# Feed-forward part of a transformer layer rebuilt as seven products of quarter matrices, on eight cores

## The chip, the cores and the metric

The kernel runs on one Trainium2 chip, on all 8 of its cores. Each core does the whole layer for one of 8 batch elements, so there is no traffic between cores. The metric is the device time of the slowest core in microseconds (us), lower is better.

## The reference

One layer on `x` of 8 x 2048 x 1024 in float32: causal attention in which keys and values come from one weight matrix and the queries are `x` itself, then a feed-forward part with a token shift, each followed by a layer norm.

```python
kv = x @ W.T;  K, V = kv[..., :d], kv[..., d:]
scores = einsum('bqd,bkd->bqk', x, K) + mask
x = _layernorm(x + (x + einsum('bqk,bkd->bqd', softmax(scores), V)))
...
x_prev = concatenate([zeros, x[:, :-1, :]], axis=1)
xr = mu_r * x + (1.0 - mu_r) * x_prev
xk = mu_k * x + (1.0 - mu_k) * x_prev
r = sigmoid(einsum('btc,dc->btd', xr, W_r))
k_act = square(relu(einsum('btc,dc->btd', xk, W_k)))
x = _layernorm(x + r * einsum('btc,dc->btd', k_act, W_v))
```

Per core this is three products of 2048 x 1024 x 1024 for the feed-forward part, two for K and V, and the causal half of two of 2048 x 2048 x 1024.

## The kernel before

Every float32 operand is held as two bf16 halves, a high part (a cast on ScalarE) and a low part (value minus high part, on VectorE, helper `minus`, L501). A product is three matmuls, high x high, high x low and low x high, `triple`, lines L317 to L319. The five engine programs are written out by hand; each runs its list in order and waits on semaphores.

**Projection.** Sixteen steps `ss` of 96 matmuls make K and V for four blocks `tt` of 512 tokens. Results go to PSUM banks 0 to 3 or 4 to 7 in turn, are split by `high_p` and `low_p`, and step `ss + 2` waits for `low_p(ss)`. Inputs come through NST = 6 staging buffers `STG` of 256 KB: SyncE (SP) issues load n once the cast of load n - 6 is done (L199).

**Attention.** Rows of 128 queries, q = 15 down to 0. TensorE flips the probabilities (L388, `flip_p`), does the scores of row q - 1, and then probabilities times V of row q (L474 to L479), with the normalized row q + 1 flipped in between (L397, `flip_x`). VectorE has row maxima (`row_max`), the low halves of the flipped probabilities (`low_p_t`), the end of the row before (`attn_rows`: L576, L578 and the variance; `normal`, L568), and, by the tables CASTS, MIXES and TILES, at the end of some rows the casts of later operands and the token mixes. GpSimd makes the token difference (`change`, L273) in `X1T`, 1/sqrt of the variance (L262), and issues the stores of `x1` and its transpose `x1t`.

**Feed-forward.** `ffn_tile(g)`, 96 tiles of 24 matmuls: for each block of 512 tokens 8 tiles of keys, 8 of the gate, 8 of values. All three weights stay in SBUF as bf16 halves (`FK`, `FR`, `FV`). The first tiles are put between the last attention rows: TILES = {3: (0, 1), 2: (1, 2), 1: (2, 4), 0: (4, 6)}. The first tile on `XR` waits for all its mixes (`v_mix`) and for `FR`. Each tile's PSUM bank is freed by one operation of ScalarE or VectorE. After the last tile: L667 gate times value, L671 residual, L561 to L564 variance, L262, L568, store.

Of the kernel before, what the change touches and what calls it, by code (L numbers as in the profile page):

```python
# [18 lines left out]
NST = 6  # L19


def build_program():
# [13 lines left out]
    x1t_d = nc.dram_tensor("x1t", [D, S], F32, kind="Internal").ap()  # L36
# [10 lines left out]
    oA, oB, oC, oD, oE = 0, 32 * KB, 64 * KB, 96 * KB, 128 * KB  # L47
    oF = 160 * KB
    oG = oF + 16 * KB + 32
    oST = oG + 16 * KB  # L50
    oX = oST + NST * 2 * KB
    oM = oX + 2 * KB
# [10 lines left out]
    STG = [at(f"STG{i}", [128, 512], F32, oST + i * 2 * KB) for i in range(NST)]  # L63
# [4 lines left out]
    XTS = [at(f"XTS{i}", [128, 512], F32, oD + 24 * KB + i * 2 * KB) for i in range(2)]  # L68
    MA = [at(f"MA{i}", [128, 512], F32, o) for i, o in enumerate((oD + 20 * KB, oD + 22 * KB, oX))]

    FK, FR, FV = hilo("FK", 8, 1024, oC), hilo("FR", 8, 1024, oB), hilo("FV", 8, 1024, oA)
    XK, XR = hilo("XK", 8, 512, oE), hilo("XR", 8, 512, oE + 16 * KB)
    X1T = at("X1T", [128, 8 * 513], F32, oF).rearrange("p (c w) -> p c w", w=513)
    KA = hilo("KA", 8, 512, oG)
    R = at("R", [128, 4 * 1024], F32, oD).rearrange("p (c w) -> p c w", w=1024)
    X1 = [at(f"X1_{i}", [128, 1024], F32, oD + 16 * KB + i * 4 * KB) for i in range(3)]
    KT = [at(f"KT{i}", [128, 512], F32, oD + 28 * KB + i * 2 * KB) for i in range(2)]
    MB = [at(f"MB{i}", [128, 512], F32, oST + i * 2 * KB) for i in range(3)]
# [16 lines left out]
    nc.const_aps.register(F32, 0.0, CONST0.ap())  # L95

# [11 lines left out]
    ld_xt = sem("ld_xt")  # L108
    ld_x1, st_y = ([sem(f"{n}{i}") for i in range(3)] for n in ("ld_x1", "st_y"))

    pe_p, pe_s, pe_t, pe_pv, pe_f = sem("pe_p"), sem("pe_s"), sem("pe_t"), sem("pe_pv"), sem("pe_f")
# [4 lines left out]
    v_mx, v_mix, v_sq, v_ka = sem("v_mx"), sem("v_mix"), sem("v_sq"), sem("v_ka")  # L116
    v_v, v_y, v_init = sem("v_v"), sem("v_y"), sem("v_init")

    a_st, a_p, a_pt, a_exp = sem("a_st"), sem("a_p"), sem("a_pt"), sem("a_exp")
    a_xt, a_mh, a_r, a_k, a_kh = sem("a_xt"), sem("a_mh"), sem("a_r"), sem("a_k"), sem("a_kh")  # L120

    g_rs, g_d, g_zero = sem("g_rs"), sem("g_d"), sem("g_zero")
# [3 lines left out]
    def chunk(n):  # L126

        def xs(tt, cc, x):
            return x0_d[cc * 128:(cc + 1) * 128, tt * 512:(tt + 1) * 512], x[0][:, cc, :], x[1][:, cc, :]

        def ws(d, h, cc, w):
            c = slice(h * 512, (h + 1) * 512)
            return d[cc * 128:(cc + 1) * 128, c], w[0][:, cc, c], w[1][:, cc, c]

        cc = n % 8
        if n < 24:
            return xs(0, n // 3, XP[0]) if n % 3 == 0 else ws(wk_d, n % 3 - 1, n // 3, WK)
# [13 lines left out]
    MIXES = {9: (0, 3), 8: (3, 6), 7: (6, 8), 1: (8, 10), 0: (10, 13)}
    TILES = {3: (0, 1), 2: (1, 2), 1: (2, 4), 0: (4, 6)}
# [9 lines left out]
    def first(q):  # L162

        return sum(G(p) for p in range(q + 1, NQ))
# [4 lines left out]


    def t_p(q, g):
        return first(q) + 2 * max(0, NQ - 2 - q) + g

    def t_x(q, i):
        return (t_p(q - 1, 0) + G(q - 1) if q > 0 else 70) + i

    t_kind = {t_p(q, g): ("p", first(q) + g) for q in range(NQ) for g in range(G(q))}
    t_kind.update({t_x(q, i): ("x", 2 * (NQ - 1 - q) + i) for q in range(NQ) for i in range(2)})

    def mix_dst(n):  # L180

        return (XK if n // 8 % 2 == 0 else XR), n % 8, (MUK if n // 8 % 2 == 0 else MUR)

    def mtmp(n):
        return (MA if n < 24 else MB)[n % 3]


    def bank(g):
        return 1 + g % 3 if g < 8 else (3, 0, 6, 7, 1, 2, 4, 5)[g % 8]

    def gate_tile(j):

        return j % 4, j // 4


    def sync_program(sy):
        def load(n):
# [10 lines left out]
        for n in range(4, 86):  # L208
            load(n)
# [13 lines left out]
        for n in range(86, N_WV):  # L223
            load(n)
# [624 lines left out]
```

## Time and profile before

| quantity | value |
|---|---|
| median of 3 runs | 1291.97 us (1273.01, 1291.97, 1403.23) |
| the profiled execution's own time | 1272.16 us |
| its span, slowest core (core 5) | 1270.6 us |
| spans of the eight cores | 1262.6 to 1270.6 us |
| granted TensorE clock, mean by core | 0.986 to 0.990 of full |
| TensorE busy | 1224.5 us, 96% |
| VectorE, ScalarE, GpSimd busy | 38%, 21%, 11% |

Time and span of the profiled execution differ by 1.56 us, which lies around the span. In the trace a matmul's duration includes its way through the array, so the distance from one start to the next is what it costs, not its duration.

### The profile page before, as it was taken

To read this page: it belongs to the slowest core of one execution; us is meant where nothing else is said; L and a number is where in the kernel's file an instruction comes from. 1 tells how busy PE (TensorE), PEld (TensorE's weight loads), DVE (VectorE), ACT (ScalarE), POOL (GpSimd) and SP (SyncE) were. 2 spreads that over 40 slices of the span, in tenths; PEclk is the share of its full clock that TensorE was granted. 3 is DMA by queue.
4 is the path that set the end of the run, shared out by engine and by line. 5 is a ranking of instruction groups with operands and counts; after the bars stand their busy time and mean duration, and the time that the engine had idled before them with its cause. 6 is when DMAs were issued, how large, how long until landed. Compare 5 with 4: busy or idle time off the path is not lost.

```text
span 1270.6 us, 15768 instructions; the slowest of 8 cores (1262.6 to 1270.6 us)
## 1 busy us (share of the span) xinstructions
PE 1224.5 (96%) x5880; PEld 579.0 (46%) x5880; DVE 481.3 (38%) x810; ACT 271.2 (21%) x514; POOL 139.9 (11%) x165
## 2 busy tenths in 40 slices
PE   7999999999999999999989996799999999999997
PEld 3444444444445554555445553344444444444443
DVE  4532121010112232332475667367432832382024
ACT  4431121010112121221233332341221122112100
POOL 0000000000000011111231223222111211120000
PEclk9999999999999999999989998899999999999999
DMA  7622020000101021323144661452300230021002
GB/s 207 179 67 67 1 67 1 1 1 1 34 1 34 17 84 50 83 84 117 50 119 133 186 194 51 149 150 83 117 1 1 84 116 1 1 100 35 1 1 83
DMA packets 36172, 87.17 MB, mean 69 GB/s; under 512 B 4096, under 2 KB 4352, under 8 KB 36096
## 3 DMA queue, kind: packets, MB, share of 16 engines
q1 hardware_dynamic: 28928, 60.98, 16.7%
q0 software_dynamic: 7168, 25.17, 6.0%
q8 instruction: 48, 0.79, 0.3%
q14 instruction: 28, 0.23, 0.1%
HBM read 60.97 MB, written 25.17 MB: 68 GB/s over the span
## 4 chain that ended last, share of the span: by engine, by line
PE 88%; DVE 5%; issue 2%; ACT 2%; DMA 1%; POOL 1%; DVEq 0%; POOLq 0%; ACTq 0%; SPq 0%
PE ps L317 24%; PE ps L318 24%; PE ps L319 24%; PE ps L474 2%; PE ps L475 2%; PE ps L478 2%; PE ps L477 2%; PE ps L476 2%; PE ps L479 2%; DMA X1T<-x1t 1%; DVE MA L586 1%; PE ps L388 1%; PE ps L397 1%; POOL MA L273 1%; DVE BN L561 1%
## 5 line engine op out<-in xcount | busy, mean ns | idle before, releaser
L317 PE MATMUL ps<-FRH,XRH 128*128 128x512 bf16 x256 | 98.7, 386 | 15.2 <-DVE XRL L501 11.5
L318 PE MATMUL ps<-FRL,XRH 128*128 128x512 bf16 x256 | 98.7, 385 | 0.0
L319 PE MATMUL ps<-FRH,XRL 128*128 128x512 bf16 x256 | 98.3, 384 | 0.0
L317 PE MATMUL ps<-FVH,KAH 128*128 128x512 bf16 x256 | 97.0, 379 | 0.0
L318 PE MATMUL ps<-FVL,KAH 128*128 128x512 bf16 x256 | 97.0, 379 | 0.0
L319 PE MATMUL ps<-FVH,KAL 128*128 128x512 bf16 x256 | 97.0, 379 | 0.0
L319 PE MATMUL ps<-XKH,FKL 128*128 128x512 bf16 x256 | 97.0, 379 | 0.0
L318 PE MATMUL ps<-XKL,FKH 128*128 128x512 bf16 x256 | 97.0, 379 | 0.0
L317 PE MATMUL ps<-XKH,FKH 128*128 128x512 bf16 x256 | 97.0, 379 | 0.0
L262 POOL TENSOR_TENSOR RS<-VE,NEGH 128x1 f32<-128x1 f32 x32 | 23.3, 727 | 406.5 <-DVE VE L564 406.5
L721 ACT ACTIVATE PROB<-ps,NEGM 128x512 f32<-128x512 f32 (+3 forms) x40 | 24.8, 622 | 194.7 <-DVE NEGM L545 194.7
L273 POOL TENSOR_TENSOR MB<-X1T 128x512 f32<-128x512 f32 x40 | 47.5, 1199 | 130.6 <-DVE XKL L501 91.2
L501 DVE SCALAR_TENSOR_TENSOR PT<-PT,ps 128x512 bf16<-128x512 bf16 (+3 forms) x40 | 23.2, 604 | 89.6 <-ACT PT L729 89.6
L667 DVE TENSOR_TENSOR R<-R,ps 128x512 f32<-128x512 f32 x32 | 22.0, 687 | 90.2 <-PE ps L319 90.2
L258 POOL DMA_DIRECT2D Z<-xtok x16 | 9.1, 566 | 343.0 <-PE ps L319 342.3
L317 PEld LDWEIGHTS ps<-FRH,XRH 128*128 128x128 bf16 x256 | 25.4, 99 | 47.1 <-issue 18.0
L289 POOL DMA_DIRECT2D x1t<-XTS x32 | 24.5, 766 | 191.6 <-ACT XTS L736 190.7
L604 DVE TENSOR_TENSOR KT<-KT 128x512 f32<-128x512 f32 x32 | 22.8, 711 | 60.1 <-ACT KT L747 60.1
L542 DVE TENSOR_REDUCE MX<-ps 128x1 f32<-128x512 f32 (+3 forms) x40 | 24.5, 611 | 51.3 <-PE ps L319 49.7
L805 ACT ACTIVATE R<-ps 128x512 f32<-128x512 f32 x32 | 19.1, 596 | 103.0 <-PE ps L319 103.0
L741 ACT CAST XRH<-MB 128x512 bf16<-128x512 f32 x24 | 14.8, 618 | 121.3 <-DVE MB L586 121.3
L319 PEld LDWEIGHTS ps<-FRH,XRL 128*128 128x128 bf16 x256 | 25.4, 99 | 31.3 <-issue 1.9
(249 smaller groups left out, 2467.2 us busy)
## 6 DMA issues: line engine op xcount, KB each, us to landing
STG<-x SPq DMA_DIRECT2D x56, 256.0 KB, 6.0
Z<-xtok POOLq DMA_DIRECT2D x16, 512.0 KB, 6.1
x<-Z POOLq DMA_DIRECT2D x16, 512.0 KB, 3.0
x1t<-XTS POOLq DMA_DIRECT2D x32, 256.0 KB, 3.1
X<-x SPq DMA_DIRECT2D x16, 512.0 KB, 3.8
y<-X SPq DMA_DIRECT2D x16, 512.0 KB, 2.6
X1T<-x1t SPq DMA_DIRECT2D x3, 2052.0 KB, 14.0
STG<-wk SPq DMA_DIRECT2D x16, 256.0 KB, 5.7
```

The source lines that it names most:

```text
L273: gp.tensor_tensor(mtmp(n), X1T[:, cc, 1:513], X1T[:, cc, 0:512], op=ALU.subtract).then_inc(g_d, 1)
L289: gp.dma_start(out=dst, in_=XTS[i].rearrange("p (c s) -> p c s", s=128)).then_inc(st_xt[i], 16)
L317: te.matmul(out, a[0], b[0], start=at_first, stop=False)
L318: te.matmul(out, a[0], b[1], start=False, stop=False)
L319: return te.matmul(out, a[1], b[0], start=False, stop=at_last)
L474: te.matmul(PS[6], ph, vh[:, j, 0:512], start=beg, stop=False)
L475: te.matmul(PS[7], ph, vh[:, j, 512:1024], start=beg, stop=False)
L476: te.matmul(PS[6], ph, vl[:, j, 0:512], start=False, stop=False)
L477: te.matmul(PS[7], ph, vl[:, j, 512:1024], start=False, stop=False)
L478: te.matmul(PS[6], pl, vh[:, j, 0:512], start=False, stop=end)
L479: mm = te.matmul(PS[7], pl, vh[:, j, 512:1024], start=False, stop=end)
L721: sc.activation(out=PROB[:, g * 512:g * 512 + w], in_=PS[g][:, 0:w], func=AF.Exp, bias=NEGM, scale=1.0, accum_out=Z4[:, g:g + 1]).then_inc ...
```

## The change

**Products.** The contraction, the rows and the columns of each 1024-wide product are halved. Per stage and half of the block (n = 2b + u, 24 of them) seven products of quarters replace eight; `product(n, k)` is 24 matmuls of 128x512, or in the key stage 48 of 128x256. The results are added up from PSUM on VectorE (`u2`, `u3`, `u4`, `quarter`).

**Stages.** The feed-forward part now runs all key blocks (b = 0 to 3), then all gate blocks, then all value blocks. The squared keys and the gate go to device memory (`ka`, `r`) and come back.

**Weights.** Seven combinations of weight quarters, as halves, are made by `weight_unit`, 12 units of 128 rows: 8 in the projection, 4 in attention rows 12 to 9. They are stored to `wc` and loaded by stage in 7 slots (`load_slot`).

**Inputs.** Of each piece, four parts are cast as they are (768 columns hold the three first), and four sums (`sums`, on GpSimd, 4 additions of 128x256) are cast as 128x1024.

**Order.** The attention rows run 15 to 7, 3, 6, 2, 5, 1, 4, 0. The first two products stand ahead of the last row's values, and wait for their pieces tile by tile. `attn_rows` now comes ahead of the probabilities' low halves; the casts of sums come behind these. NST is 5. The last row is finished by halves of 512 columns.

```diff
-NST = 6
+NST = 5
+ORDER = [15, 14, 13, 12, 11, 10, 9, 8, 7, 3, 6, 2, 5, 1, 4, 0]
+    UNITS = {12: 8, 11: 9, 10: 10, 9: 11}
+    MIXES = {ORDER[8 + x]: x for x in range(4)}
+    PROD = {1: (2, 0), 2: (0, 1), 3: (6, 2), 4: (1, 6), 5: (3, 3), 6: (4, 4), 7: (5, 5)}
+    ORDER_P = (1, 2, 6, 7, 5, 4, 3)
...
+        def load(n):
+            if n >= NST:
+                old = CH[n - NST]
+                if old[0] == "st":
+                    sy.wait_ge(v_st, plain(n - NST))
+                elif old[0] == "m":
+                    sy.wait_ge(v_mx, old[2] + 1)
+                elif n - NST == N[f"u{old[2]}"][0]:
+                    store_unit(old[2])
...
+        def sums(x):
...
+            step(gp.tensor_tensor(s1, a21, a22, op=ALU.add))
+            gp.tensor_tensor(s3, a11, a21, op=ALU.subtract)
+            step(gp.tensor_tensor(s2, s1, a11, op=ALU.subtract))
+            gp.tensor_tensor(s4, a12, s2, op=ALU.subtract).then_inc(g_s, 1)
...
+        def product(n, k):
...
+            if turn < 4:
+                te.wait_ge(a_exp, 40)
+            elif turn < 6:
+                te.wait_ge(v_z, 16)
+            else:
+                product_read(te.wait_ge, (turn - 6) // 7, ORDER_P[(turn - 6) % 7])
+            ac = AC[b % 2]
+            for t in range(2 if s == 0 else 1):
+                for p in range(4):
+                    if k in (1, 2) and u == 0 and t == 0:
+                        te.wait_ge(v_ac, 8 * b + 2 * p + 1)
...
+        def weight_1(u):
...
+            step(ve.tensor_tensor(UT[:, 0:512], b12, b11, op=ALU.subtract))
+            ve.tensor_tensor(UT[:, 512:1024], b22, UT[:, 0:512], op=ALU.subtract).then_inc(v_ut, 1)
+            for m, f in enumerate((b11, b21, b22)):
+                ve.wait_ge(a_w, 5 * u + m + 1)
+                minus(ol[:, m, :], oh[:, m, :], f)
...
+            step(minus(flat(ol, 3, 5), flat(oh, 3, 5), UT))
+        def weight_2(u):
+            ve.tensor_tensor(UT[:, 0:512], b22, b12, op=ALU.subtract)
+            ve.tensor_tensor(UT[:, 512:1024], b21, UT[:, 512:1024], op=ALU.subtract).then_inc(v_ut, 1)
...
+            minus(flat(ol, 5, 7), flat(oh, 5, 7), UT).then_inc(v_w, 1)
...
         for q in ORDER:
+            prev, nxt = before(q), after(q)
+            if prev is not None:
+                attn_rows(prev)
+            low_p_t(q, 0)
...
+            if prev in MIXES:
+                low_unit(MIXES[prev])
...
+            if q in MIXES:
+                mix(MIXES[q])
```

TensorE, one key tile. Before, the first six of its 24 rows at `ffn_tile(0)` (eight such triples for one bank):

```order
L317 MATMUL ps1<-XKH_99,FKH_93 128x512
L318 MATMUL ps1<-XKL_100,FKH_93 128x512
L319 MATMUL ps1<-XKH_99,FKL_94 128x512
L317 MATMUL ps1<-XKH_99,FKH_93 128x512
L318 MATMUL ps1<-XKL_100,FKH_93 128x512
L319 MATMUL ps1<-XKH_99,FKL_94 128x512
```

After, the beginning of a key product (four such triples for each half of a bank; `AC` are the pieces, `WA` a slot of weights):

```order
L637 MATMUL ps0<-AC00H_114,WA0_100 128x256
L638 MATMUL ps0<-AC00L_115,WA0_100 128x256
L639 MATMUL ps0<-AC00H_114,WA0_100 128x256
L637 MATMUL ps0<-AC01H_116,WA0_100 128x256
L638 MATMUL ps0<-AC01L_117,WA0_100 128x256
L639 MATMUL ps0<-AC01H_116,WA0_100 128x256
```

The triples are the same, half as wide, and of half the depth.

SyncE in the projection. Before, its queue holds nothing but loads of `STG` there (x0 here, wk and wv ahead of it):

```order
L200 DMA STG3_80<-wv 128x512
L200 DMA STG4_81<-x0 128x512
L200 DMA STG5_82<-x0 128x512
L200 DMA STG0_77<-x0 128x512
L200 DMA STG1_78<-x0 128x512
```

After, each unit of weights has four loads (`fk` or `fr`) and two stores (`UO` are the made halves) in the same queue; the stores of unit 2 stand ahead of the last three loads of unit 3:

```order
L342 DMA STG1_78<-fk 128x512
L342 DMA STG2_79<-fk 128x512
L342 DMA STG3_80<-fk 128x512
L330 DMA wc<-UO65536H_90 128x7x512
L330 DMA wc<-UO65536L_91 128x7x512
L342 DMA STG4_81<-fk 128x512
L342 DMA STG0_77<-fk 128x512
L342 DMA STG1_78<-fk 128x512
L342 DMA STG2_79<-fr 128x512
```

The two stores stand between one unit's end and the next one's inputs.

VectorE at the end of attention. Before, between the flipping of row 1's results and those of row 0 (`Z0`):

```order
L568 TENSOR_SCALAR Z1_87<-Z1_87,MV0_126,RS0_130 128x1024
L604 TENSOR_TENSOR KT0_110<-KT0_110 128x512
L501 SCALAR_TENSOR_TENSOR KAL_105<-KAH_104,KT0_110 128x512
L604 TENSOR_TENSOR KT1_111<-KT1_111 128x512
L501 SCALAR_TENSOR_TENSOR KAL_105<-KAH_104,KT1_111 128x512
L586 SCALAR_TENSOR_TENSOR MA1_91<-MA1_91,MUR_117,X1T_103 128x512
L586 SCALAR_TENSOR_TENSOR MA2_92<-MA2_92,MUR_117,X1T_103 128x512
L501 SCALAR_TENSOR_TENSOR XRL_102<-XRH_101,MA1_91 128x512
L586 SCALAR_TENSOR_TENSOR MA0_90<-MA0_90,MUR_117,X1T_103 128x512
L501 SCALAR_TENSOR_TENSOR XRL_102<-XRH_101,MA2_92 128x512
L501 SCALAR_TENSOR_TENSOR XRL_102<-XRH_101,MA0_90 128x512
L576 SCALAR_TENSOR_TENSOR Z0_86<-ps6,RZ0_123,Z0_86 128x512
```

After, in the same place (row 4 is now the last but one; `OUT0` is the first quarter of a result, L970 a mix for the second block):

```order
L945 TENSOR_SCALAR Z0_85<-Z0_85,MV0_163,RS0_167 128x1024
L1018 TENSOR_TENSOR OUT0_138<-SN0_135,ps1 128x512
L954 SCALAR_TENSOR_TENSOR Z1_86<-ps6,RZ1_161,Z1_86 128x512
L956 SCALAR_TENSOR_TENSOR Z1_86<-ps7,RZ1_161,Z1_86 128x512
L970 SCALAR_TENSOR_TENSOR TP1_131<-TP1_131,MUK_155,STG4_81 128x512
```

Ten operations on keys and mixes are gone from there; one addition stands in their place, and the mixes come behind `Z`.

## Rows read from the trace of the kernel before

**Rows 1.** The page, busy time of the engines.

```profile
PE 1224.5 (96%) x5880; PEld 579.0 (46%) x5880; DVE 481.3 (38%) x810; ACT 271.2 (21%) x514; POOL 139.9 (11%) x165
```

**Rows 2.** Windows by stage: us, busy of each engine, PEclk, DMA share, GB/s.

```profile
0.00:343.00 343.00, 335.18 (x1540) 151.43 (x1541) 82.72 (x129) 75.63 (x129) 0.20 (x4) 1.00 0.20 55
343.00:716.50 373.50, 363.62 (x1884) 186.08 (x1882) 138.10 (x267) 78.67 (x178) 44.88 (x65) 0.99 0.26 77
716.50:830.00 113.50, 93.42 (x458) 45.67 (x457) 69.10 (x122) 39.18 (x75) 29.98 (x36) 0.91 0.47 142
830.00:1262.40 432.40, 432.28 (x2003) 195.82 (x2001) 187.51 (x288) 77.77 (x133) 64.30 (x59) 1.00 0.17 54
1262.40:1270.60 8.20, 0.00 (x0) 0.00 (x0) 3.84 (x7) 0.00 (x0) 0.55 (x1) 0.74 0.16 64
```

**Rows 3.** TensorE's groups by shape: nine such in the feed-forward part.

```profile
L317 PE MATMUL ps<-FRH,XRH 128*128 128x512 bf16 x256 | 98.7, 386 | 15.2 <-DVE XRL L501 11.5 <-DVE FRL L501 3.7
```

**Rows 4.** Timeline of TensorE, scores of row 13: start, duration, operation.

```profile
409.92 0.38 PE L317 MATMUL ps<-K0H,XP3H 128*128 128x512 bf16 x1
...
425.46 0.27 PE L317 MATMUL ps<-K3H,XP3H 128*128 128x256 bf16 x1
...
427.97 0.27 PE L319 MATMUL ps<-K3H,XP3L 128*128 128x256 bf16 x1
```

**Rows 5.** Timeline of TensorE, where it had been idle: the bracket has the idle time before.

```profile
7.83 0.59 PE L317 MATMUL ps<-XP0H,WKH 128*128 128x512 bf16 x1 [7.83 <-DVE WKL L501]
...
365.68 1.94 PE L388 MATMUL ps<-IDN,PROB 128*128 128x128 f32 x8 [2.60 <-ACT PROB L721]
...
622.19 0.38 PE L474 MATMUL ps<-V0H,PT 128*128 128x512 bf16 x1 [1.05 <-DVE Z L578]
...
650.43 0.59 PE L474 MATMUL ps<-V0H,PT 128*128 128x512 bf16 x1 [4.85 <-DVE Z L578]
...
723.46 0.41 PE L397 MATMUL ps<-IDN,Z 128*128 128x128 f32 x2 [1.49 <-DVE Z L568]
...
772.08 0.66 PE L397 MATMUL ps<-IDN,Z 128*128 128x128 f32 x2 [2.81 <-DVE Z L568]
...
797.67 0.58 PE L317 MATMUL ps<-FRH,XRH 128*128 128x512 bf16 x1 [11.54 <-DVE XRL L501]
...
825.31 0.38 PE L317 MATMUL ps<-FRH,XRH 128*128 128x512 bf16 x1 [3.71 <-DVE FRL L501]
```

**Rows 6.** Windows on TensorE: us, busy, PEclk, DMA share, GB/s.

```profile
652.00:656.00 4.00, 4.00 (x12) 0.58 0.14 59
800.00:804.00 4.00, 4.00 (x15) 0.74 0.52 145
0.00:50.00 50.00, 42.17 (x183) 1.00 0.79 213
```

**Rows 7.** Groups by shape on VectorE and ScalarE: count, busy us, mean ns, idle before.

```profile
L501 DVE SCALAR_TENSOR_TENSOR WKL<-WKH,STG 128x512 bf16<-128x512 bf16 x16 | 10.7, 691 | 3.1 <-ACT WKH L689 3.1
L604 DVE TENSOR_TENSOR KT<-KT 128x512 f32<-128x512 f32 x32 | 22.8, 711 | 60.1 <-ACT KT L747 60.1
L501 DVE SCALAR_TENSOR_TENSOR XQ0L<-XQ0H,STG 128x512 bf16<-128x512 bf16 x8 | 11.1, 1444 | 14.2 <-ACT XQ0H L689 14.2
...
L689 ACT CAST WKH<-STG 128x512 bf16<-128x512 f32 x16 | 9.8, 617 | 3.9 <-DMA STG<-wk 3.4
```

**Rows 8.** The instructions on `X1T`: count, ns min/median/max, first and last start.

```profile
L273 POOL TENSOR_TENSOR MB<-X1T x40: 1033/1117/1537, 846.6 to 1133.4; 128x512 f32<-128x512 f32 x40
...
L586 DVE SCALAR_TENSOR_TENSOR MA<-MA,MUK,X1T x16: 737/740/2436, 612.4 to 846.3; 128x512 f32<-128x512 f32 x16
```

**Rows 9.** The page, DMA issues: KB each, median us to landing.

```profile
STG<-x SPq DMA_DIRECT2D x56, 256.0 KB, 6.0
...
X1T<-x1t SPq DMA_DIRECT2D x3, 2052.0 KB, 14.0
```

More of the change, by code:

```diff
@@ L74, in build_program, with seven @@
[L74 to L78, printed above, removed]
+    XTS = [at(f"XTS{i}", [128, 512], F32, oD + 20 * KB + i * 2 * KB) for i in range(2)]
+    UT = at("UT", [128, 1024], F32, oX)
+    def seven(name, w, off):
+        return at(name, [128, 7 * w], BF16, off).rearrange("p (m w) -> p m w", w=w)
@@ L171, in t_p @@
     def t_p(q, g):
-        return first(q) + 2 * max(0, NQ - 2 - q) + g
+        return T_EV["p", q, g]
     def t_x(q, i):
[L175 to L185, printed above, removed]
@@ new lines, in pair_free, with store_unit @@
+    def pair_free(wait, x):
+        if x >= 6:
+            wait(v_ac, 2 * (x - 1))
+        elif x >= 4:
+            wait(pe_pv, first(4) + 2)
+        elif x > 0:
+            wait(v_ac, 2 * x)
+    def sync_program(sy):
+        def store_unit(u):
+            sy.wait_ge(v_w, u + 1)
+            o, p = unit_out(u), u % 4
+            for h in range(2):
+                dst = wc_d[u // 4, h, :, p * 128:(p + 1) * 128, :].rearrange("m p w -> p m w")
+                sy.dma_start(out=dst, in_=o[h]).then_inc(st_w, 16)
@@ L372, in scores, with exp_before @@
                 mm.then_inc(pe_s, 1)
+        def exp_before(q, g):
+            p = before(q)
+            while G(p) <= g:
+                p = before(p)
+            return first(p) + g + 1
         def bank_free(e):
@@ L454, in tensor_program @@
                 flip_p(q, 1)
-            if q > 0:
-                scores(q - 1)
-            if q in TILES:
-                for g in range(*TILES[q]):
-                    ffn_tile(g)
+            if q == 0:
+                product(0, 1)
+                product(0, 2)
+            else:
+                scores(after(q))
+            prev = before(q)
             for g in range(n):
@@ new lines, in vector_program @@
+        for b in range(1, 8):
+            x, n = 4 * b + 4, 2 * b
+            more = x < 32
+            if more:
+                mix(x)
+            quarter(b, 0)
+            low_unit(x)
+            u2(n)
+            if more:
+                mix(x + 1)
+            u3(n)
+            quarter(b, 1)
+            u4(n)
+            low_unit(x + 1)
+            quarter(b, 2)
+            if more:
+                mix(x + 2)
+            quarter(b, 3)
+            if more:
+                mix(x + 3)
+            low_unit(x + 2)
+            quarter(b, 4)
+            u2(n + 1)
+            low_unit(x + 3)
+            u3(n + 1)
+            quarter(b, 5)
+            u4(n + 1)
+            quarter(b, 6)
+            quarter(b, 7)
@@ L685, in scalar_program @@
+        ve.wait_ge(g_rs, 32)
+        for h in range(2):
+            part = x1[:, h * 512:(h + 1) * 512]
+            ve.tensor_scalar(part, part, MV[1][:, 0:1], RS[1], op0=ALU.subtract, op1=ALU.mult).then_inc(v_y, 1)
     def scalar_program(sc):
```

1145 lines of the change are left out of this document (776 added, 369 removed).

## The prediction

> **What bounds the kernel now.** I read the page first: TensorE is busy 96% of the span, the next engine 38% [rows 1]. Then the windows by stage: TensorE is full from 830 us to the last matmul at 1262.4, nearly full in projection and attention, and only 93.4 of 113.5 us are busy in the change-over from attention to feed-forward, where the granted clock also falls to 0.91 [rows 2]. Behind the last matmul come 8.2 us. So the time is a floor of matmuls plus the places where TensorE waits. The timeline gives both: starts are 0.2158 us apart for 128x512 (409.92 to 425.46, 72 of them) and 0.1091 us for 128x256 (425.46 to 427.97, 23 intervals) [rows 4]; and the idle times say who was late [rows 5].
>
> **Products.** The feed-forward part has nine groups of 256 matmuls [rows 3]: 2304 x 0.2158 = 497.2 us. By the order of the changed kernel, gate and value products have 16 x 7 x 12 = 1344 of 128x512 and the key products 8 x 7 x 24 = 1344 of 128x256: 290.0 + 146.6 = 436.7 us. That is 60.5 us less, all on the path, since no other engine is near its limit. A half-width matmul costs 0.0012 us more than half a full one, 1.6 us in all, which is in the sum.
>
> **What must stay hidden beside the products.** A product takes 5.2 us, a block of fourteen 72.6 us. A bank is taken again six products later, so a reader has some 26 us before TensorE waits. VectorE has per block in the key stage 8 mixes, 14 additions from PSUM, 4 casts of 768 and 4 of 1024 columns; at 0.69 us for 512 columns and in proportion for the wider ones [rows 7] that is 6 + 9.7 + 9.6 = 25 us of 72.6. ScalarE has 4 x (0.9 + 1.2) for casts and some 18 x 0.6 for the rest, 19 us [rows 7]. GpSimd has 8 differences at 1.12 us and 16 additions of 256 columns, which the trace does not show; between half of a 512-column one and all of it, 0.56 to 1.12 us [rows 8], they make 18 to 27 us. I take the half. In the value stage GpSimd has 8 residual additions in place of the differences, and no more. All fit by a factor of two or more. I cost them at nothing; if that cover were gone (a chain of mix, sums, two casts late by a block's time), it would be paid eleven times.
>
> **End of attention.** Six waits stand between 622 and 826 us: 1.05, 4.85, 1.49, 2.81, 11.54, 3.71, together 25.4 us [rows 5]. All name VectorE, and the order shows why: the mixes, key halves and weight casts of the first feed-forward block stood there between one row's results and the next. At the lower clock, 12 and 15 matmuls ran in 4 us where 18.5 fit [rows 6]; with the time from 650.43 and 797.67 to those windows at half speed, the two cost 2.2 and 2.0 us. For those behind 2.81 and 3.71 us of idleness I estimate 1 and 1.5 from these. So 32 us lie there. The changed kernel has its weights made long before; short rows alternate with long ones, so that scores (1.294 us for each 128 keys, 6 x 0.2158) cover the maxima and the exponential of the row ahead; and 10.4 us of products stand ahead of row 0's values. I followed the four iterations that carry a mix (rows 7, 3, 6, 2) with durations of rows 7 and 8. VectorE's tail there is casts 2.4 us, then two GpSimd differences 2.2 us that wait for these casts, then two mixes 1.5 us. In row 6 it ends 2.5 us before the values of that row are through. In row 2 it ends 2.6 us behind them; with the 1.5 us of `attn_rows` and 0.7 of `low_p_t` ahead of row 5's values, and 2.6 + 0.7 us of scores and flips beside it, TensorE waits about 1.5 us. Row 4, with only 1.4 us of scores beside it, gives 0.5. So of 32 us 30 are gained; what is late next there is VectorE again, by 2 us.
>
> For the additions that GpSimd now makes beside it: `XQ0L` took 1.44 us against 0.69, and a mix once 2.44 against 0.74, while GpSimd worked in the same stretch [rows 7, 8]. The Trainium skill, "SBUF — State Buffer", section "Who interferes with whom", says that a VectorE operation with two SBUF inputs and a GpSimd one that reads SBUF exclude each other, the later one waiting for the whole of the earlier. The doubled durations agree with it. By it each of the 24 GpSimd operations of those four rows (8 differences, 16 additions) could hold up VectorE by its own length, an estimate of 18 us of delay, of which TensorE would see only what falls in rows 2 and 5, some 5 us; that lies in the range.
>
> **Weights by units.** New work in the projection, where VectorE is busy 24% [rows 2]. A unit on VectorE: 4 additions x 0.71, 3 casts x 0.69, 2 of double width x 1.38, and one wait for a double cast of ScalarE, 1.23 [rows 7]: 8.9 us. Moved into SP's queue: two stores of 0.92 MB after each unit, ahead of the last three loads (0.79 MB) of the next. 2.62 MB at 213 GB/s, as in the first 50 us [rows 6], is 12.3 us. Period 21.2 us against 20.7 us (96 x 0.2158) for the projection step beside it. Behind VectorE's wait for those loads stands `low_p` of the next step, which may be late by about 15 us before step ss + 2 waits. Half a microsecond a unit over seven units is hidden. Queued too are the loads of the fourth token block, whose casts wait for the last stores into the same memory: I find them ready about when step 12 starts, and put 2 us there. The other bound is the transfer of 2052 KB in 14.0 us [rows 9], 150 GB/s: 17.5 + 8.9 = 26.4, 5.7 us late per unit, 40 over seven, of which 15 are hidden: 25 us. I take 2, since the issue pattern in the first 50 us is nearest (loads alone, one behind another). The stores' pieces of 1 KB in device memory occur nowhere in this trace.
>
> The Trainium skill, "DMA: Bandwidth & Descriptors", section "Specifications", gives line rate from 512 B up and 358 GB/s per core. By it the 2.62 MB would be an estimated 7.3 us and the period 16 us, with nothing lost; no run here has shown that rate for such a mix.
>
> The four units in attention rows 12 to 9 are split round a row maximum. A long row has 11 to 15 us of scores and as much of values: 8.9 us on VectorE fit, no cost.
>
> **Staging, start and end.** With 5 buffers of STG instead of 6 and 6.0 us to land [rows 9], plus 1.3 for the two casts [rows 7], a load comes each 1.5 us; TensorE needs one each 1.7 us (24 matmuls, 5.2 us, for three of them). The first wait of 7.83 and the one of 2.60 ahead of the first flip stay [rows 5]. I put 3 us for small waits here and at the joints of stages. At the end, an addition from PSUM (0.7) is added, half of the statistics and half of the normalization are taken off (0.7 + 0.4): 8.2 stays 8.
>
> **Sum.** 1270.6 - 60.5 - 32 + 2 (rows 5 and 4) + 2 (fourth block) + 3 = 1185.1 us of span, plus the 1.56 that lie around the span: 1187 us. The executions shown have a median of 1291.97 and a lowest of 1273.01; the sum is against the profiled one, 1272.16, which agrees with the lowest, and a changed kernel's median should be compared with that.
>
> **Rivals.**
> 1. *The units' transfers set the projection's pace.* For: the period is already 0.5 us over the step. Against: 15 us of slack, 213 GB/s reached by loads. Price 10 to 30 us: 1197 to 1217. Chance 0.15.
> 2. *The waits at the end of attention come back in a new place* (VectorE behind GpSimd in rows 3 to 5, or the casts of the first queries' block in row 8, which I find only 3 us early). For: the doubled durations. Price half of what I let go, 16 us, up to all of it: 1203 to 1219. Chance 0.13.
> 3. *The products do not run dense*: bank waits, late sums, or key products slower than 0.109 us per matmul. A wait of 1 us for each of 168 products would cost 168 us; for one in four, 42 us: 1229. Against: 26 us of slack each. Chance 0.05. Were it so throughout, the change would not do what it says.
> 4. *Slower than before.* The same mechanism as 1 with its threshold: the forecast is beaten by 85 us only if seven units are late by (85 + 15) / 7 = 14.3 us each, a period of 35 us, that is 2.62 MB in 26 us, under 100 GB/s. Then 1273 and more. The slowest large transfer in the rows has 150 GB/s. Chance 0.03.
>
> **How the numbers follow.** Forecast 0.64, alone 1176 (none of the 7 us of new waits, and the small waits under 0.6 us gone too) to 1196. Rivals 1 and 2 together go up to 1219. The range 1172 to 1220 leaves out rivals 3 and 4 and some tails. A difference under 2%, 25 us, could hardly be told from none. Faster by over 2% means under about 1247: 0.94; within 2%: 0.04; slower: 0.02.
>
> **What would show it.** In the profile after: 128x512 starts 0.216 us apart and 128x256 0.109 in the feed-forward part, which lasts about 437 us plus flips; TensorE above 97% busy; no idle time of 4 us or more between the start and the last matmul; DMA share roughly twice as high, with a GpSimd busy share near 20%; steps 4 to 12 of the projection without a wait on `low_p`. Wrong would be: TensorE idle with VectorE as releaser at steps 9 to 12 (rival 1), idle time at rows 3 to 4 (rival 2), or waits ahead of products beyond the first block (rival 3).

## The result and the profile after

The changed kernel takes 1224.74 us, median of six executions (1219.72 to 1229.9), against 1291.9 for the kernel before (lowest 1272.08). The ratio is 0.9625, 95% interval 0.9562 to 0.9687. All ratios, and the times of the experiments, leave out slow executions (over 1.5% above the fastest of the same kernel, or one die over 1% longer at a lower granted clock), without which the kernel before had 1268.5 to 1273.2 us beside every experiment. The profiled execution took 1224.53 us, with a span of 1223.0. That is faster by over 2%, but some 37.5 us above the forecast of 1187 and outside the range of 1172 to 1220.

The page of the changed kernel, busy time and then the chain that ended last:

```profile
PE 1166.1 (95%) x6264; PEld 614.1 (50%) x6264; DVE 624.4 (51%) x901; ACT 409.0 (33%) x673; POOL 369.4 (30%) x420
...
PE 59%; POOL 12%; DMA 10%; issue 7%; DVE 6%; ACT 3%; SPq 1%; DVEq 0%; POOLq 0%; ACTq 0%
```

TensorE's share has fallen from 96 to 95% [rows 1], and GpSimd has 369 us of work instead of 140. The chain is what to look at: only 59% of it is TensorE. The last matmul was held, step after step, by a chain that runs through GpSimd, DMA and VectorE.

Windows by stage (columns as in [rows 2]):

```profile
0.00:343.00 343.00, 335.84 (x1550) 152.03 (x1551) 137.67 (x202) 105.15 (x170) 3.51 (x9) 1.00 0.44 123
343.00:716.50 373.50, 368.43 (x1933) 190.14 (x1931) 164.91 (x315) 92.50 (x192) 59.43 (x86) 1.00 0.41 120
716.50:830.00 113.50, 104.36 (x894) 88.18 (x893) 73.14 (x97) 42.86 (x67) 67.53 (x70) 0.97 0.57 171
830.00:1060.00 230.00, 217.00 (x1258) 122.10 (x1257) 149.77 (x166) 86.25 (x121) 130.60 (x135) 0.99 0.53 157
1060.00:1215.00 155.00, 140.49 (x635) 61.61 (x633) 97.43 (x117) 80.30 (x122) 106.88 (x118) 0.99 0.56 195
1215.00:1223.00 8.00, 0.00 (x0) 0.00 (x0) 1.50 (x5) 1.97 (x3) 1.43 (x4) 0.50 0.33 131
```

Projection and attention went as forecast: TensorE lost 7.2 us in the first stage and 5.1 in the second, where it had lost 7.8 and 9.9 [rows 2]. In the change-over 104.4 of 113.5 us are busy instead of 93.4. Behind 830 us it is the other way round. There TensorE had been full (432.28 of 432.40); now it stands 13.0 us of the next 230 and 14.5 of the last 155, 3.1 of these behind the last matmul, which ends at 1211.9.

The chain of waits, by what TensorE waited for (us in total, times, longest):

```profile
PE ps L637 <- DVE OUT L1018: 18.3, 15, 3.9
PE ps L637 <- DVE WKL L825: 7.2, 1, 7.2
PE ps L637 <- DVE AC13L L825: 4.9, 4, 3.9
PE ps L637 <- DVE SN L1018: 4.4, 6, 1.2
PE ps L728 <- DVE Z L945: 4.2, 1, 4.2
...
PE ps L719 <- ACT XTS L1256: 2.5, 5, 0.7
PE ps L637 <- DVE AC03L L825: 1.1, 2, 0.7
```

`L637` is the first matmul of a product. `OUT` and `SN` are the sums that VectorE adds up out of PSUM, and a wait for them is a wait for a bank; `AC03L` and `AC13L` are the last mixed, summed and cast piece of a block. Together 18.3 + 4.9 + 4.4 + 1.1 = 28.7 us, in 27 waits: this is the loss. In the place of the six old waits at the end of attention [rows 5] stands one that is worth naming, 4.2 us for `Z`, and it is a new one.

These are the numbers of the slowest core, 7. The others had spans from 1206.4 to 1219.8 us, and on the fastest, core 3, the same four entries come to 18.6 us. So the pattern is on every core, and its size is not: the slowest core sets the time.

**Where a bank comes free late.** VectorE's waits between 735 and 1215 us, then GpSimd's:

```profile
DVE OUT L1018 <- DMA r<-OUT: 41.6, 13, 6.0
DVE OUT L1018 <- DMA ka<-OUT: 20.9, 9, 4.7
```

```profile
POOL SU L540 <- DVE TP L970: 68.3, 18, 10.6
```

VectorE, half idle by its busy share (51%), waited 62.5 us for stores of `OUT`. There are two `OUT` buffers: the addition of one quarter waits for the store of the quarter two earlier. The timeline of VectorE shows what that holds up (start, duration, operation, idle time ahead of it in brackets):

```profile
902.30 0.68 DVE L1018 TENSOR_TENSOR OUT<-SN,ps 128x512 f32<-128x512 f32 x1
907.71 0.69 DVE L1018 TENSOR_TENSOR OUT<-SN,ps 128x512 f32<-128x512 f32 x1 [4.73 <-DMA ka<-OUT]
908.32 1.41 DVE L970 SCALAR_TENSOR_TENSOR TP<-TP,MUR,STG 128x512 f32<-128x512 f32 x2
```

And the chain that ended last, the pieces between 904 and 927 us (start, duration, engine, tile):

```profile
904.56 3.54 DMA ka<-OUT
908.32 1.42 DVE TP L970 x2
909.93 0.74 POOL SU L540
910.80 0.72 POOL SU L541
911.53 1.41 POOL SU L542
...
914.04 2.04 POOL TP L520 x2
...
923.05 1.05 ACT AC11H L1279
924.20 1.84 DVE AC11L L825
```

Read it as a loop. VectorE adds a quarter; ScalarE passes over it twice; the store takes 3.5 us; only then may VectorE add the quarter two later, and behind that addition, in program order, stands the next piece's mix (`TP` L970). GpSimd's four sums wait for the mix, ScalarE's cast for the sums, VectorE's low half for the cast. The same two rows of VectorE, an `OUT` after 0.70 us for ScalarE's `SN`, come at 868.26 and at 910.42: a round of 42.2 us for fourteen products. TensorE needs 14 x 12 x 0.2158 = 36.3 us for them. (From 1098 us on, in the value stage, where no `OUT` is stored, eight short waits add up to 5.0 of the 28.7 us. No store can hold them up there; experiments 6 and 11 come back to them.)

**The new stall at the end of attention.** GpSimd's timeline, and the operation of TensorE that waited last:

```profile
714.92 0.58 POOL L571 DMA_DIRECT2D x<-Z  x1 [3.42 <-DVE Z L945]
...
726.97 0.56 POOL L499 DMA_DIRECT2D Z<-xtok  x1 [7.56 <-DMA x<-Z]
```

```profile
729.29 0.63 PE L728 MATMUL ps<-IDN,Z 128*128 128x128 f32 x4 [4.22 <-DVE Z L945]
```

The store of `x` took some 11.5 us to land; its median is 3.2. SP had issued the four loads of the first two weight slots (2 MB) at 713.98 and three loads of `x1t` behind them. GpSimd stood 7.56 us for the landing before it could load the next `Z`, and behind that load in its order stands the 1/sqrt that VectorE's `Z` waits for. On the eight cores the same store took 7.6 to 11.5 us, and TensorE's waits for `Z` came to 1.2 to 4.2 us.

### The profile page after: what moved, and what is told of

It is laid out like the page before. It is cut to its first block, busy times and chain, and to the rows that moved or that the text cites. A ratio compares the mean times of both kernels' runs of the same rounds, so it can differ in the third digit from the quotient of the medians.

```text
span 1223.0 us, 18516 instructions; the slowest of 8 cores (1206.4 to 1223.0 us)
## 1 busy us (share of the span) xinstructions
PE 1166.1 (95%) x6264; PEld 614.1 (50%) x6264; DVE 624.4 (51%) x901; ACT 409.0 (33%) x673; POOL 369.4 (30%) x420
## 4 chain that ended last, share of the span: by engine, by line
PE 59%; POOL 12%; DMA 10%; issue 7%; DVE 6%; ACT 3%; SPq 1%; DVEq 0%; POOLq 0%; ACTq 0%
PE ps L637 15%; PE ps L639 15%; PE ps L638 15%; DMA r<-OUT 4%; POOL SU L542 3%; POOL SU L541 3%; PE ps L791 2%; PE ps L792 2%; PE ps L796 2%; PE ps L794 2%; PE ps L795 2%; PE ps L793 2%; POOL SU L540 2%; DVE TP L970 2%; DMA STG<-x1t 2%
## 5 line engine op out<-in xcount | busy, mean ns | idle before, releaser
L1018 DVE TENSOR_TENSOR OUT<-SN,ps 128x512 f32<-128x512 f32 x96 | 65.5, 684 | 78.8 <-DMA r<-OUT 41.6
L520 POOL TENSOR_TENSOR TP<-STG 128x512 f32<-128x512 f32 x64 | 75.0, 1193 | 24.8 <-DMA STG<-x1t 13.3
L540 POOL TENSOR_TENSOR SU<-TP 128x256 f32<-128x256 f32 x48 | 39.3, 819 | 100.4 <-DVE TP L970 68.3
L555 POOL TENSOR_TENSOR X<-X,RR 128x512 f32<-128x512 f32 x31 | 46.8, 1518 | 33.0 <-DVE RR L1062 33.0
L509 POOL TENSOR_TENSOR RS<-VE,NEGH 128x1 f32<-128x1 f32 x32 | 18.2, 569 | 109.6 <-DVE VE L941 107.4
L1018 DVE TENSOR_TENSOR SN<-SN,ps 128x512 f32<-128x512 f32 x72 | 48.8, 678 | 3.9 <-PE ps L639 3.1
L542 POOL TENSOR_TENSOR SU<-SU,TP 128x256 f32<-128x256 f32 x48 | 49.1, 1024 | 0.0
L543 POOL TENSOR_TENSOR SU<-TP,SU 128x256 f32<-128x256 f32 x48 | 44.7, 931 | 7.2 <-POOL SU L542 0.4
L541 POOL TENSOR_TENSOR SU<-TP 128x256 f32<-128x256 f32 x48 | 42.5, 886 | 7.2 <-POOL SU L540 0.4
L1336 ACT ACTIVATE OUT<-OUT 128x512 f32<-128x512 f32 x32 | 20.1, 629 | 67.0 <-DVE OUT L1018 67.0
L970 DVE SCALAR_TENSOR_TENSOR TP<-TP,MUK,STG 128x512 f32<-128x512 f32 x32 | 34.5, 1116 | 7.7 <-POOL TP L520 7.7
L1332 ACT ACTIVATE OUT<-OUT 128x512 f32<-128x512 f32 x32 | 20.0, 626 | 40.3 <-DVE OUT L1018 40.3
L637 PE MATMUL ps<-XP0H,WKH 128*128 128x512 bf16 x64 | 24.9, 389 | 7.2 <-DVE WKL L825 7.2
L970 DVE SCALAR_TENSOR_TENSOR TP<-TP,MUR,STG 128x512 f32<-128x512 f32 x32 | 31.0, 1008 | 0.0
```

The source lines that it names most:

```text
L520: gp.tensor_tensor(tp(x)[:, e * 512:(e + 1) * 512], st[:, 1:513], st[:, 0:512], op=ALU.subtract).then_inc(g_d, 1)
L540: step(gp.tensor_tensor(s1, a21, a22, op=ALU.add))
L541: gp.tensor_tensor(s3, a11, a21, op=ALU.subtract)
L542: step(gp.tensor_tensor(s2, s1, a11, op=ALU.subtract))
L543: gp.tensor_tensor(s4, a12, s2, op=ALU.subtract).then_inc(g_s, 1)
L555: gp.tensor_tensor(X1[g % NROW][:, c], X1[g % NROW][:, c], RR[g % NROW][:, c], op=ALU.add).then_inc(g_add, 1)
```

## The experiments

**1. No stores of `ka` and `r`.** The loads that read them back read other memory of the same size, and the buffers' waits are on ScalarE instead. The profile is read on core 7.

```diff
-                sy.dma_start(out=dst, in_=OUT[o % 2]).then_inc(st_o[o % 2], 16)
-            elif 2 <= o < 64:
-                ve.wait_ge(st_o[o % 2], 16 * (o // 2))
+            elif 2 <= o < 34:
+                ve.wait_ge(a_ka, o - 1)
```

> Left out: the 64 stores of squared keys and gates; the loads that would read them back read x instead, at the same sizes. VectorE then waits for ScalarE's last use of the buffer OUT, not for the landing of its store. Theory S (VectorE is held by the landing of stores, 62 us of its waits in the feed-forward part, and mixes, GpSimd's sums and the casts queue up behind it): most of TensorE's 28 us of idle time between the products goes, 0.975 to 0.985 of the changed kernel, about 1195 us. Theory G (the length of GpSimd's sums sets the loop): the waits come back behind the sums, 0 to 6 us gained. Theory P (VectorE and GpSimd hold each other up): as G.

Measured: 1192.09, 1195.42 and 1196.41 us, 28 to 33 below the changed kernel. Of TensorE's five longest entries none is a wait for `OUT`; beside the start and the flips, these are left:

```profile
PE ps L628 <- DVE WKL L816: 7.2, 1, 7.2
...
PE ps L628 <- DVE AC13L L816: 2.5, 1, 2.5
...
PE ps L719 <- DVE Z L936: 1.4, 2, 1.0
```

So taking the stores away is enough to win back nearly all, as Theory S said. But this kernel stores less as well (64 x 256 KB), so it does not tell the wait from the load on memory.

**2. Short sums.** From the seventh piece on, GpSimd adds 32 columns of 256; the products then work on stale sums.

```diff
-            a12, a22, a11, a21 = (tp(x)[:, k * 256:(k + 1) * 256] for k in range(4))
+            v = 32 if x >= 6 else 256
+            a12, a22, a11, a21 = (tp(x)[:, k * 256:k * 256 + v] for k in range(4))
```

> From the seventh piece on GpSimd's four additions are made over 32 columns in place of 256; the rest of the sums is stale data. Theory G: the loop is shorter by some 2.5 us for each of four pieces in a block, the idle time between products goes, about 1197 us. Theory P: the same, and the mixes on VectorE fall from 1.06 to 0.75 us and the casts of sums from up to 1.9 to 1.22 us. Theory S: the stores still hold VectorE, 5 to 12 us gained, 1210 to 1218 us.

Measured: 1192.51, 1193.38 and 1195.1 us; TensorE waits 4.5 us for `OUT` in the profiled one. Yet VectorE waits for the stores longer than ever:

```profile
DVE OUT L1019 <- DMA r<-OUT: 51.0, 13, 7.4
...
DVE OUT L1019 <- DMA ka<-OUT: 21.9, 9, 7.2
```

Theory S had given 1210 to 1218 here and missed; Theory G's 1197 is near. So the stores do not have to be touched: this loop is relieved at either of two legs, and what VectorE then waits for mostly no longer reaches TensorE. Neither leg is the one cause.

**3. Sums that only write.** Four fills of 704 columns take the place of the four sums, the products' data are constants.

```diff
-            step(gp.tensor_tensor(s1, a21, a22, op=ALU.add))
+            step(gp.memset(su(x)[:, 0:704], 0.5))
```

> GpSimd's four additions per piece are replaced by four fills of 704 columns, about as long (0.7 us each), that read nothing; the sums are constants. It tells theory P from theory G. P: durations on VectorE fall to 0.75 and 1.22 us while GpSimd is as busy as before, and 8 to 20 us are gained. G: 0 to 4 us gained. S: 0 to 8 us.

```profile
L540 POOL MEMSET SU<- 128x704 f32 x44 | 30.2, 686 | 103.5 <-DVE TP L970 70.9 <-DMA TP<-ka 32.6
```

Measured: 1192.77, 1197.18 and 1199.11 us. A fill takes 0.686 us each time; a sum in the changed kernel takes 0.727 at the median, up to 1.7, and a low half on VectorE is stretched too, as the tiles' views of the changed kernel show (ns min/median/max):

```profile
L540 POOL TENSOR_TENSOR SU<-TP x44: 717/727/1706, 751.6 to 1173.2; 128x256 f32<-128x256 f32 x44
...
L825 DVE SCALAR_TENSOR_TENSOR AC10L<-AC10H,SU x6: 1241/1825/2292, 756.1 to 1152.2; 128x1024 bf16<-128x1024 bf16 x6
```

The mean of the four sums is 819, 886, 1024 and 931 ns, together 3.66 us for 2.74 of fills: 0.9 us shorter a piece, four pieces a block. No theory gave 26 to 32 us: P had 8 to 20, G and S less. VectorE's durations fell only in part. The mixes went from 1116 and 1008 ns in the mean to 1042 and 914, but the low half `AC10L` keeps a median of 1832 ns; in the changed kernel the one at 915.32 us has GpSimd's two differences beside it (`TP` L520, 914.04 above), and these were left as they are. So this run does not tell P from G: it makes the sums shorter and frees VectorE at once.

**4. The next block's first mix ahead of the last quarter.** Nothing is left out; the first mix of each next block moves one place forward in VectorE's order, ahead of an addition that waits for a store.

```diff
+        mix(8)
...
-            if more:
-                mix(x)
+            if x + 4 < 32:
+                mix(x + 4)
```

> VectorE's mix of the next block's first piece stands ahead of the last quarter of this block instead of behind it; nothing else is changed. Theory S: the wait for the store no longer holds back GpSimd's first sums, some 3 us in each of the key and gate blocks, 8 to 15 us gained, 1208 to 1215 us. Theories G and P: under 5 us, since the loop is as long as before.

Measured: 1206.77, 1207.95, 1209.49 and 1213.72 us, some 15 us better, as Theory S said. TensorE waits 13.3 us for `OUT` (18.3 before the edit), VectorE 69.8 us for stores: the mix no longer stands behind them, but the bank still does.

**5. The kernel before with an eighth of its feed-forward left out.** The contraction runs over seven of eight chunks, which is worth as much of TensorE's time as the products of quarters are.

```diff
-            for cc in range(NCH):
+            for cc in range(NCH - 1):
```

> The kernel before, with its feed-forward contracted over seven of the eight chunks: one eighth of the feed-forward is left out, which takes from TensorE the same 60 us as the seven products do (21 matmuls of 128x512 for 24 in each group), but adds no sums, no stores or loads of ka and r, and no longer chain. It shows what that amount of TensorE's time is worth alone, in the order before. Theory A (the changed kernel lost its 28 us to a loop of stores, VectorE, GpSimd and ScalarE that the products' sums form): here TensorE stays dense, and the time falls by 58 to 62 us against the kernel before, to about 1209, with idle time of TensorE between 850 and the end below 6 us. Theory B (whatever is taken from TensorE, the engines behind it, which have less time for each group, give a third or a half of it back): it falls by only 30 to 45 us. If A holds, the part of the change that lies at the end of attention brought the rest, about 30 us.

Measured: 1221.86, 1238.37 and 1239.92 us, ratio 0.9692 (0.9611 to 0.9774); in the two longer ones cores 6 and 7 alone were some 20 us behind. The six other cores of the profiled one had 1213.0 to 1221.1, against 1262.6 to 1270.6 for the kernel before: 50 us less in the mean, not 58 to 62. From 850 us on, core 0 had no wait at all that the profile names:

```profile
830.00:1205.00 375.00, 371.36 (x1694) 168.82 (x1727) 181.98 (x284) 74.71 (x128) 67.84 (x58) 1.00 0.16 59
```

Theory A holds for the stage behind 830 us, where TensorE stays dense; its size was missed by some 10 us. Most of that is longer waits of TensorE: on cores 0 to 5 they come to 45.3 us in the mean, in the kernel before to 37.5, 8 us less. For core 0 the two change-over waits are 12.5 and 3.1 us (11.5 and 3.2 before), those for `Z` L568 6.6 (4.3 before). What remains I cannot place.

**6. Three output buffers.**

```diff
+    OUT.append(at("OUT2", [128, 16384], F32, oC + 31 * KB).rearrange("p (t s) -> p t s", s=8192)[:, :, 0:256])
...
-            elif 2 <= o < 64:
-                ve.wait_ge(st_o[o % 2], 16 * (o // 2))
+            elif 3 <= o < 67:
+                ve.wait_ge(st_o[o % 3], 16 * (o // 3))
```

> The changed kernel with three buffers for the output sums instead of two, so that VectorE's sum waits for the store three sums earlier and not two; the third one is made of two 1 KB pieces, and all three are written through a view in two halves. Nothing is left out. In the changed kernel VectorE waits 41.6 us for the stores of r and 20.9 for those of ka in the feed-forward. Theory A (the stores are one leg of a loop of about 41 us for a block of fourteen, in which TensorE needs 36.3): most of the stores' waits go, and with them two thirds of what is lost between the products, 12 to 22 us: 1203 to 1213. Theory B (the loop closes through GpSimd's sums and ScalarE's casts even without the stores): the stores' waits fall, the waits of GpSimd and ScalarE grow by as much, and the time falls by less than 8 us, 1217 to 1225.

Measured: 1199.09, 1200.05 and 1203.88 us, ratio 0.9438 (0.9416 to 0.9459): 24 us below the changed kernel, with the same work and the same traffic. VectorE waits 27.7 us for stores of `r`, the stores of `ka` are not among its ten longest entries, and TensorE is full where it had 197.7 of 210 us:

```profile
850.00:1060.00 210.00, 210.00 (x1150) 112.31 (x1148) 143.21 (x161) 80.33 (x113) 123.46 (x123) 1.00 0.60 183
```

```profile
PE ps L642 <- DVE AC13L L830: 4.9, 3, 3.3
PE ps L733 <- DVE Z L950: 3.5, 1, 3.5
PE ps L642 <- DVE OUT L1023: 2.1, 3, 1.0
```

Theory A, and more than it gave. GpSimd's sums cost 0.82 to 1.03 us each in the mean here as well, and nothing was stored less: so the wait two stores back, taken away by itself, was worth the 24 us. What is left between the products is 9.7 us: 3.3 ahead of one product of the first block, and 6.4 in eight waits from 1070 us on, in the value stage (2.1 for `OUT`, 2.0 for `SN`, 2.3 for pieces), where no `OUT` is stored. GpSimd is busy 96.0 of the 125 us from 1065 on there.

**7. Slots later.**

```diff
+        load_unit(5)
+        sy.wait_ge(v_x1, 15)
         for m in (6, 2):
             load_slot(0, m, ld_wg)
-        load_unit(5)
```

> The changed kernel with the unit of the hidden layer loaded first at the end of attention, and the four loads of the first weight slots (2 MB) held back until VectorE has made fifteen of the sixteen pieces of x1. Theory: the store of x that took 11.48 us to land at 714.9 (others 3.2) was slowed by those 2 MB, and GpSimd, VectorE and TensorE (4.22 us at 729) waited for it in turn. Then TensorE's wait for the normalised tile falls to about 1 us, and the time by 3 to 6 us: 1219 to 1222. Rival: the store was slowed by something else, or the first product now waits for its weights, and the time stays within 2 us or grows.

Measured: 1219.42 to 1228.26 us, ratio 0.9615 (0.9585 to 0.9645): no difference. The wait for `Z` is gone, and another stands in its place:

```profile
PE ps L638 <- DVE OUT L1019: 18.7, 14, 4.6
...
PE ps L638 <- DMA WA<-wc: 4.4, 1, 4.4
```

The stores of `x` land in 4.3 us at the median and 7.9 at most here, which fits the cause; the gain was nothing, since the same 2 MB, loaded later, came 4.4 us too late for the product that needs them. This is the rival.

**8. All three, 9. the first two, and 10. the slots spread.** Number 10 loads one slot behind the fourteenth piece of `x1` and one behind the fifteenth:

```diff
-        sy.wait_ge(v_x1, 15)
-        for m in (6, 2):
+        for m, k in ((6, 14), (2, 15)):
+            sy.wait_ge(v_x1, k)
             load_slot(0, m, ld_wg)
```

> The changed kernel with the three edits at once: three buffers for the output sums, the next block's first mix ahead of the last quarter (which alone brought about 15 us), and the weight slots loaded later. Nothing is left out. Theory A (one loop, each edit gives it slack, and no more than the 28 us between products and the 4.2 before them can be had): 1190 to 1200, TensorE's waits for sums below 4 us in all. Theory B (a second bound, GpSimd and VectorE slowing each other, keeps a floor): no better than the mix alone, 1205 to 1212.

> The changed kernel with three buffers for the output sums and the next block's first mix ahead of the last quarter, the weight slots loaded where the changed kernel loads them. The kernel with all three edits lost 5.5 us at 743 to the slots' loads, which came too late there. Theory A (two places are left, that one and the loop's rest): without the late loads it gets back 1 to 3 us net, since the stall for the normalised tile (4.2 us) returns in their place: 1192 to 1198 in the undisturbed executions. Rival: what is left is spread over the clock, the start and the tail, and it stays where the three edits were, 1194 to 1204.

> The same with the two weight slots' loads spread: 1 MB after the fourteenth piece of x1 and 1 MB after the fifteenth, instead of 2 MB at one of the two ends. Theory (2 MB at once either delays the store of x, which GpSimd waits for, or comes too late for the first product): both waits of TensorE between 725 and 750 fall below 2 us each, and the time is 2 to 4 us below that of the kernel with the slots loaded early, 1189 to 1195. Rival: any load in those 20 us delays the store or is delayed by it, and one of the two waits keeps 4 us.

Measured: all three 1194.28 to 1203.99 us, ratio 0.943 (0.9392 to 0.9468); without the late slots 1195.21 to 1204.28, ratio 0.9433 (0.9396 to 0.9469); spread 1194.92 to 1199.96, ratio 0.9415 (0.9382 to 0.9447). None can be told from three buffers alone (0.9416 to 0.9459). With all three, TensorE waits 5.5 us for `WA`; spread, 0.7 us:

```profile
PE ps L643 <- DVE AC13L L831: 4.2, 3, 2.5
PE ps L643 <- DVE OUT L1024: 3.2, 4, 1.3
...
PE ps L643 <- DMA WA<-wc: 0.7, 1, 0.7
```

Number 8 has its median, 1198.0, inside what Theory A gave and two executions above it, with 4.3 us of waits for sums instead of under 4. Number 9 has a median of 1198.3 and all executions but for 0.3 us inside its rival's 1194 to 1204, so it leans to the rival. The spreading does what it should for TensorE, whose waits there are below 1 us, and the time hardly shows it: 1 to 2 us between medians, less than the executions differ, with a median of 1196.5 where 1189 to 1195 was expected. The mix first, worth 15 us alone, is worth nothing that can be seen once the third buffer is there: two edits that relieve the same loop did not add.

**11. Number 9 with sums that only write** (the edit of 3).

> The kernel with three buffers and the mix first, with GpSimd's four sums of each piece replaced by four fills of 704 columns that take as long (0.69 us each) and read nothing; the products then multiply constants, which takes TensorE the same time. Theory (GpSimd and VectorE slow each other, 0.72 to 0.82 us and more, 0.74 to 1.1; but this mattered in the changed kernel only because the loop had no slack): with slack in the loop nothing more is won, within 3 us of the same kernel with its sums. Rival: the contention still costs TensorE its last waits, and it comes 4 to 8 us lower.

Measured: 1186.96, 1188.15, 1188.3 and 1188.45 us, ratio 0.9346 (0.9326 to 0.9365), some 10 us below number 9 and more than the rival gave. I was wrong: what GpSimd's sums cost still reaches TensorE when the loop has slack. It is the last waits for sums that go. Number 9 has 12.7 us of them, 7.8 in the value stage; here 0.6 is left, at 775 us, and behind it TensorE does not wait again:

```profile
PE ps L642 <- DVE WKL L830: 8.9, 1, 8.9
PE ps L733 <- DVE Z L950: 4.2, 2, 2.6
...
PE ps L642 <- DVE AC13L L830: 0.6, 1, 0.6
```

That this comes near the forecast's 1187 is no support for it: these products multiply constants. The run does not say which part of the 10 us is VectorE set free and which the shorter work (0.686 us a fill, 0.82 to 1.05 a sum in the mean in number 9). No kernel with all its sums and stores came below 1194.

## Why the prediction was wrong

**The failing step** is "A product takes 5.2 us, a block of fourteen 72.6 us. A bank is taken again six products later, so a reader has some 26 us before TensorE waits", with "All fit by a factor of two or more. I cost them at nothing". A product is 12 matmuls of 128x512, or 24 of 128x256: 2.59 us, a block 36.3, and the five products between two uses of a bank 13 us (ahead of the prediction, too, "24 matmuls of 128x512, or in the key stage 48 of 128x256" is twice the number, and so are the "10.4 us of products" ahead of row 0's values). The total in the same text was right: 16 x 7 x 12 matmuls and 8 x 7 x 24 are 168 products and 436.7 us, which twelve blocks of 72.6 would have overshot by a factor of two. The cover was never checked against it.

With the right cover the text's own figures looked different: VectorE 25 of 36.3 us, GpSimd 18 to 27 of 36.3. What that left unpriced came to 28.7 us of TensorE's waits. Measured, a block's GpSimd work in the key stage is 8 x 1.19 + 4 x 3.66 = 24 us, and VectorE is busy 136.0 of the 210 us from 850 to 1060, 27 us a round of 42. Neither is over the edge by its busy time. What was over it was their sum in a row: the sentence "if that cover were gone (a chain of mix, sums, two casts late by a block's time)" names half of the loop, and leaves out its other half, the stores behind two `OUT` buffers. I listed readers of banks and never walked from a store back to the mix that stands behind it on VectorE. Experiments 4 and 6 show that this wait is what closed the loop (15 and 24 us, with all the work in it), and 2 and 3 that the sums on GpSimd are its other leg.

**Rival 3** was this, "bank waits, late sums ... a wait of 1 us ... for one in four, 42 us: 1229". It came to 27 waits of 1.06 us in the mean, 28.7 us and 1224.7. It had 0.05, "against: 26 us of slack each", which is the same mistake. With 13 us of slack and 25 of 36.3 us it deserved a much larger chance, and a range that reaches its 1229.

**The sum against the measurement.** Without its 7 us for new waits the forecast's span is 1178.1. The profiled one adds 28.7 for the products, 4.2 for `Z`, 1.1 for `XTS` (2.5 against 1.4 in the kernel before) and 0.4 for `PT`, less 0.6 at the start (7.2 instead of 7.83), and the lower clock behind four of the longer waits. In the eight microseconds from 936, 25 matmuls ran in 6.65 busy us where 31 fit (columns: us, TensorE busy, PEclk, DMA share, GB/s):

```profile
936.00:940.00 4.00, 2.65 (x9) 0.80 0.02 4
940.00:944.00 4.00, 4.00 (x16) 0.77 0.25 92
```

Behind each of the four waits (4.2 us at 729, 3.9 at 778, 2.0 at 937, 3.9 at 1071) the first 4 us show a granted clock of 0.57 to 0.64, and behind the last two 12 and 11 matmuls where 18.5 fit: some 1.5 us a place, 6 for four, an estimate. The tail behind the last matmul adds 3.1. Together 1221.0 of 1223.0; 2 us stay unassigned.

**Step by step:**
- Products, 60.5 us less: right as matmuls. Starts are 0.1091 us apart for 128x256 and 0.2158 for 128x512 (799.75 to 800.29, five intervals, and 895.72 to 897.01, six). 28.7 us were given back.
- End of attention, 32 us gone and 2 back: the 32 right as far as the waits show, the 2 not. Rows 5 and 4 did not cost them; 4.2 us (1.2 on the core with the least) came from a place that I had put at nothing. I asked of each moved transfer what it does to its queue, not what 2 MB at once do to a 0.5 MB store on another.
- Weights by units, hidden: right. No wait stands in the projection behind the start, and the stores in 1 KB pieces did not slow it; the DMA share is 0.44, and was 0.20 [rows 2]. Rival 1 did not happen, nor did the 2 us for the fourth block.
- Rival 2 (late casts or GpSimd beside VectorE at the end of attention): not as written.
- The addition of 256 columns, "I take the half", 0.56 us: 0.73 undisturbed and 0.91 in the mean. 32 columns took 0.25 us at the median in experiment 2 (0.34 to 0.41 in the mean); the line through 0.25 and 0.73 leaves 0.18 us, an estimate, that does not shrink with the width.
- "In the value stage GpSimd has 8 residual additions in place of the differences, and no more": these took 1.52 us each in the mean, not 1.12, 20 us of small operations on the rows' statistics (L506, L509, L512) stand beside them, and GpSimd is busy 106.9 of the 155 us from 1060 on. The share over the whole span is 30%, not near 20.
- VectorE and GpSimd against each other: the rule was cited, its 18 us put beside four rows of attention, and not one was put into the feed-forward part, where the sums are. Experiment 11 took 10 us off by replacing the sums; how much of that is this effect stays open. The Trainium skill, "SBUF — State Buffer", section "Who interferes with whom", says that a VectorE operation with two SBUF inputs contends with a GpSimd one that reads SBUF, and not with one that only writes it. The traces agree in kind: both engines' operations lengthen (1241 to 2292 ns for one cast, 717 to 1706 for one sum), and fills, which read nothing, keep 0.686 us.
- The tail, "8.2 stays 8": wrong by 3 us. The last matmul ends at 1211.9, so 11.1 us follow it (11.0 to 11.3 in every other experiment on the changed kernel). The sum halved what VectorE had done there. In the chain, the last row's mean and squares now pass through ScalarE and the rest of its statistics through GpSimd (start, duration, engine, tile):

```profile
1211.66 0.23 PE ps L639
...
1212.95 1.16 ACT X L1345 x2
...
1214.48 1.25 ACT RR L1349 x2
...
1216.28 0.56 POOL RS L509
```

- "TensorE above 97% busy; no idle time of 4 us or more": 95% and one of 4.2. "Waits ahead of products beyond the first block" was named as the sign of rival 3, and it is there.

## What to carry to other kernels

Before work is called covered, multiply the time of a unit by the number of units and see that the stage's total comes out; an error of two in the cover is invisible in the sum and decides everything else. Busy shares of 65 and 56% on two engines (VectorE and GpSimd from 850 to 1060 us) say nothing where each waits for the other: walk the loop from a buffer's release (store, two passes, an addition) through whatever stands behind it in program order back to itself, and compare its length with the period, not its parts. Here the loop was 6 us too long in the round measured, one more buffer was worth 24 us over the run, and a second remedy on top of it nothing that shows.

## What the runs showed that I had not expected

- A store of 0.5 MB took some 11.5 us beside 2 MB of loads whose issue began 0.9 us ahead of it on another queue, against 3.2 at the median. Held back by some 19 us (experiment 8), the loads themselves came too late. Spread over two points, 1 MB each, they let a store of `x` still take up to 9.0 us, but TensorE waited under 1 us for either.
- A GpSimd addition of 128x256 f32 takes 0.727 us at the median, one of 128x32 0.25, a 128x704 fill 0.686.
- With a third output buffer, two thirds of what TensorE still waits for between products (6.4 of 9.7 us) lies in the value stage, where nothing is stored through that buffer. In experiment 1 none of it is there, on core 7; why, the runs do not show.
